# A transformer layer (linear attention with decay, and an expert-mixed linear layer) on eight cores: V weights by another queue, the decay set-up later, k scaled a slot ahead, and a split last chunk

## What is computed

```python
xn = layernorm(x)
# attention: H = 8 heads of DK = 64
q = phi(xn @ W_Q.T); k = phi(xn @ W_K.T); v = xn @ W_V.T       # phi(u) = elu(u) + 1
S = gamma * S + k_t v_t^T;  z = gamma * z + k_t                # per token and head
out_t = (S q_t) / (z q_t + 1e-6)
y = (out * sigmoid(xn @ W_g.T + b_g)) @ W_O.T
# linear layer with low-rank experts: 8 experts of rank 4, the best 2
f = xn @ W_lin.T + b_lin + sum_k softmax_weight_k * (xn @ left_k) @ right_k
return x + y + f
```

## Time and profile before

| | us |
|---|---|
| median of 3 runs (lowest, highest) | 260.21 (259.84, 260.92) |
| the profiled execution | 260.27 |
| its span, the slowest core (core 3) | 259.2 |
| span of the other cores | 256.0 to 258.8 |
| TensorE busy | 236.6 (91%) |
| VectorE, ScalarE, POOL busy | 162.0, 75.5, 61.7 |
| granted clock of TensorE, all cores | 1.000 |

### The profile page before, as it was taken

How to read it: one execution, slowest core, us unless ns; L and a number is a source line. 1 busy time by engine, 2 the same in 40 slices (tenths; PEclk the granted TensorE clock), 3 DMA queues, 4 the chain that set the end, 5 groups by cost and what they waited for, 6 DMA issues and landing times.

```text
span 259.2 us, 5279 instructions; the slowest of 8 cores (256.0 to 259.2 us)
## 1 busy us (share of the span) xinstructions
PE 236.6 (91%) x1688; PEld 116.9 (45%) x1688; DVE 162.0 (63%) x425; ACT 75.5 (29%) x128; POOL 61.7 (24%) x99
## 2 busy tenths in 40 slices
PE   0238999999989999999999999999999999999995
PEld 0124354454545555454444455444545454445442
DVE  3743667658848678666555657556656776677522
ACT  2653766476163432314132021112110201000000
POOL 0790300012144421405050403021304030333000
PEclk9999999999999999999999999999999999999999
DMA  5999999999998046342435122223231315243423
GB/s 147 237 153 263 250 167 188 252 174 177 232 199 266 3 116 192 61 164 61 164 41 170 37 82 83 101 82 104 82 124 63 121 63 181 82 153 104 154 106 137
DMA packets 20366, 35.86 MB, mean 138 GB/s; under 512 B 12210, under 2 KB 12530, under 8 KB 20084
## 3 DMA queue, kind: packets, MB, share of 16 engines
q1 hardware_dynamic: 17444, 24.89, 32.0%
q0 software_dynamic: 2896, 10.64, 21.7%
HBM read 32.00 MB, written 8.39 MB: 156 GB/s over the span
## 4 chain that ended last, share of the span: by engine, by line
PE 85%; DMA 6%; DVE 3%; issue 2%; ACT 2%; DVEq 0%; ACTq 0%; POOLq 0%
PE PJ L367 27%; PE L L389 17%; PE L L433 9%; PE PJ L360 8%; DMA wv_sb<-wv 5%; PE PJ L389 4%; PE L L367 3%; PE PJ L433 2%; PE SY L381 2%; DMA x_sb<-x 2%; PE SY L405 2%; PE T L419 1%; PE SY L409 1%; PE T L338 1%; PE T L427 1%
## 5 line engine op out<-in xcount | busy, mean ns | idle before, releaser
L389 PE MATMUL L<-wlin_sb,xnfm 128*128 128x512 bf16 x208 | 49.2, 379 | 0.0
L325 POOL TENSOR_SCALAR S_blk<-S_sb,small_s 128x260 bf16<-128x260 f32 x30 | 28.6, 969 | 82.7 <-DVE S_sb L827 82.5
L389 PEld LDWEIGHTS L<-wlin_sb,xnfm 128*128 128x128 bf16 x208 | 20.0, 98 | 24.4 <-issue 1.0
L656 DVE TENSOR_SCALAR e_sb<-e_sb 128x512 bf16<-128x512 bf16 x32 | 9.7, 302 | 30.7 <-ACT e_sb L898 30.7
L898 ACT ACTIVATE e_sb<-PJ 128x512 bf16<-128x512 f32 x28 | 16.5, 593 | 40.5 <-PE PJ L367 39.4
L367 PE MATMUL PJ<-xnfm,wk_sb 128*128 128x512 bf16 x112 | 26.6, 380 | 1.2 <-ACT th_g L905 1.2
L874 ACT ACTIVATE xn_tm<-x_sb,nmr,rstd 128x1024 bf16<-128x1024 f32 x16 | 19.9, 1242 | 25.4 <-POOL nmr L281 23.9
L433 PE MATMUL L<-wo_sb,ygfm 128*128 128x512 bf16 x104 | 26.7, 379 | 0.0
L367 PE MATMUL PJ<-xnfm,wg_sb 128*128 128x512 bf16 x112 | 26.6, 379 | 0.0
L367 PE MATMUL PJ<-xnfm,wq_sb 128*128 128x512 bf16 x112 | 26.6, 380 | 0.0
L360 PE MATMUL PJ<-wv_sb,xnfm 128*128 128x512 bf16 x96 | 23.7, 389 | 2.5 <-DMA wv_sb<-wv 2.5
(11 more groups left out here) (122 smaller groups left out, 336.7 us busy)
## 6 DMA issues: line engine op xcount, KB each, us to landing
ro_sb<-x SPq DMA_DIRECT2D x16, 512.0 KB, 3.4
out<-ro_sb SPq DMA_DIRECT2D x15, 512.0 KB, 2.7
x_sb<-x SPq DMA_DIRECT2D x10, 512.0 KB, 8.4
x_sb<-x POOLq DMA_DIRECT2D x6, 512.0 KB, 21.6
wlin_sb<-wlin POOLq DMA_DIRECT2D x1, 2048.0 KB, 38.5
wv_sb<-wv POOLq DMA_DIRECT2D x4, 256.0 KB, 12.7
wq_sb<-wq POOLq DMA_DIRECT2D x2, 512.0 KB, 18.5
wk_sb<-wk POOLq DMA_DIRECT2D x2, 512.0 KB, 25.4
```

The costliest lines, as they stand in the source:

```text
L325: GP.tensor_scalar(S_blk[:, :].rearrange("p (q w) -> p q w", q=4)[:, :, 65 * e : 65 * e + 65], S_sb[:, :].rearrange("p (q w) -> p q w", q= ...
L389: TE.matmul(lb(c, n)[:, :], xnk(k, c), wlin_sb[:, D * k + 512 * n : D * k + 512 * n + 512], start=False, stop=False)
L656: VE.tensor_scalar(e_sb[:, 512 * i : 512 * i + 512], e_sb[:, 512 * i : 512 * i + 512], 1.0, None, ALU.min).then_inc(dv_m, 1)
```

## The change

1. **V's weights.** V is loaded uncast, in two halves, by SyncE's queue, into the space of `wlin_sb` (seen as f32), between and behind x chunks 2 and 3. VectorE casts it in four pieces into `wv_sb` (`cast_wv`, semaphore `dv_cast`). POOL waits for the first half before it issues the load of Q's first half. W_lin, whose space is borrowed, waits for the four casts; its load and that of W_O are issued ahead of `gC` and `dpk` instead of behind. TensorE takes V's matmuls in another order.
2. **The decay set-up** is spread behind the V and Q work: the mask exponents behind the last Q feature, `dpq` behind the Q exps, `masks` behind the normalisation of chunk 7. The statistics of chunks 4 and 5 come earlier.
3. **k scaled a slot ahead.** From slot 4 on, unless a block begins, `ktm_sb` of chunk c+1 is computed in slot c, ahead of the gate multiply.
4. **Output sums.** In slots 13 to 15 the second output sum of the chunk c-3 stands behind the masks, instead of at the end of the slot before.
5. **The last chunk** is computed in parts of 512, 256 and 256 columns, in the banks PJ0, PJ1 and SY0, with a sum and a store each.

```diff
+LAST = ((0, 512), (512, 256), (768, 256))
...
+    wv32 = wlin_sb[:, :].bitcast(F32)
...
+        def load_wv(hf):
+            o = 4 * FH * hf
+            SY.dma_start(wv32[:, o : o + 4 * FH],
+                         wv_d[:, o : o + 4 * FH]).then_inc(d_wv[hf], 16)
+
         load_x(0)
         load_x(1)
         SY.dma_start(ident[:, :], ident_d[:, :]).then_inc(d_id, 16)
         load_x(2)
+        load_wv(0)
         load_x(3)
+        load_wv(1)
...
     def pool_program():
         GP.memset(mhalf[:, :], -0.5).then_inc(po_ini, 1)
-        GP.wait_ge(d_x[0], 16)
-        for i in range(4):
-            o = 2 * FH * i
-            GP.dma_start(wv_sb[:, o : o + 2 * FH], wv_d[:, o : o + 2 * FH]).then_inc(d_wv[i], 16)
+        GP.wait_ge(d_wv[0], 16)
         wload_half(wq_sb, wq_d, 0, d_wq)
...
+        GP.wait_ge(dv_cast, 4)
+        wload(wlin_sb, wlin_d, d_wl)
+        wload(wo_sb, wo_d, d_wo)
         GP.wait_ge(po_ini, 1)
         GP.wait_ge(ac_dec, 3)
...
-        wload(wlin_sb, wlin_d, d_wl)
-        wload(wo_sb, wo_d, d_wo)
...
+    def last_part(c, o, w, bank):
+        n = o // 512
+        ro_ = ((c // 4) % 2) * 512 + 128 * (c % 4)
+        TE.matmul(bank[:, 0:w], thr[64 * n : 64 * n + 64, ro_ : ro_ + 128],
+                  right_sb[64 * n : 64 * n + 64, o - 512 * n : o - 512 * n + w],
+                  start=True, stop=False)
+        for k in range(KCH):
+            TE.matmul(bank[:, 0:w], xnk(k, c), wlin_sb[:, D * k + o : D * k + o + w],
+                      start=False, stop=False)
+        for j in range(4):
+            ins = TE.matmul(bank[:, 0:w], yg(c)[:, 128 * j : 128 * j + 128],
+                            wo_sb[:, D * j + o : D * j + o + w],
+                            start=False, stop=(j == 3))
+        ins.then_inc(pe_o, 1)
...
+    def cast_wv(i):
+        o = 2 * FH * i
+        VE.wait_ge(d_wv[i // 2], 16)
+        VE.tensor_copy(wv_sb[:, o : o + 2 * FH], wv32[:, o : o + 2 * FH]).then_inc(dv_cast, 1)
...
+            if c < 4 or s == 0:
+                ktm(c)
+            if c == 0:
+                VE.wait_ge(ac_mk, 1)
             VE.wait_ge(pe_sc, c + 1)
             VE.tensor_tensor(A_sb[:, 0:512], SYb[0][:, :], masks[:, 0:512], ALU.mult)
             VE.tensor_tensor(A_sb[:, 512:1024], SYb[1][:, :], masks[:, 512:1024],
                              ALU.mult).then_inc(dv_mask, 1)
+            if c > NCH - 4:
+                outv(lo - 1, 1)
...
             if c < NCH - 1:
                 qt(c + 1)
+            if c >= 4 and s < 3:
+                ktm(c + 1)
...
-            if lo >= 0:
+            if lo >= 0 and (c < NCH - 4 or c == NCH - 1):
                 outv(lo, 1)
```

More of the change, by code:

```diff
@@ L129, in build_core @@
     ring4 = [PJ[0], PJ[1], L[0], L[1]]
+    lastb = [PJ[0], PJ[1], SYb[0]]
     sem = nc.alloc_semaphore
@@ L138, in build_core @@
     d_lg = sem("d_lg")
-    d_wv, d_wq, d_wk, d_wg = ([sem(f"d_wv{i}") for i in range(4)], [sem("d_wqa"), sem("d_wqb")],
+    d_wv, d_wq, d_wk, d_wg = ([sem("d_wva"), sem("d_wvb")], [sem("d_wqa"), sem("d_wqb")],
                               [sem("d_wka"), sem("d_wkb")], [sem("d_wga"), sem("d_wgb")])
@@ L145, in build_core @@
     pe_av, pe_st, pe_ytr, pe_o = sem("pe_av"), sem("pe_st"), sem("pe_ytr"), sem("pe_o")
+    dv_cast = sem("dv_cast")
     dv_ini, dv_st, dv_bn, dv_xev = sem("dv_ini"), sem("dv_st"), sem("dv_bn"), sem("dv_xev")
@@ L251, in sp_program @@
         c = NCH - 1
-        for n in range(2):
+        for n, (o, w) in enumerate(LAST):
             SY.wait_ge(dv_out, 2 * c + n + 1)
-            SY.dma_start(out_d[128 * c : 128 * c + 128, 512 * n : 512 * n + 512],
-                         ro(c)[:, 512 * n : 512 * n + 512]).then_inc(d_o[c], 16)
+            SY.dma_start(out_d[128 * c : 128 * c + 128, o : o + w],
+                         ro(c)[:, o : o + w]).then_inc(d_o[c], 16)
         for c in range(NCH - 1):
             SY.wait_ge(d_o[c], 16)
-        SY.wait_ge(d_o[NCH - 1], 32)
+        SY.wait_ge(d_o[NCH - 1], 16 * len(LAST))
     def wload(dst, srcd, s):
@@ L486, in pe_program @@
         TE.wait_ge(dv_xev, 1)
+        for i in range(2):
+            TE.wait_ge(dv_cast, i + 1)
+            vproj(0, ring4[0], 2 * i, 2 * i + 2)
         xtr(2)
         TE.wait_ge(dv_xev, 2)
[L489 to L498, removed]
+        vproj(1, ring4[1], 0, 4)
+        TE.wait_ge(dv_xev, 3)
+        vproj(2, ring4[2], 0, 4)
+        for i in range(2, 4):
+            TE.wait_ge(dv_cast, i + 1)
+            vproj(0, ring4[0], 2 * i, 2 * i + 2)
+        xtr(3)
+        vproj(1, ring4[1], 4, 8)
+        vproj(2, ring4[2], 4, 8)
+        TE.wait_ge(dv_xev, 4)
+        vproj(3, ring4[3])
         TE.wait_ge(d_wq[0], 16)
@@ L629, in pe_program @@
                 gproj(c)
[L630 to L634, removed]
+        lo = NCH - 2
+        right_pair(lo)
+        for n in range(2):
+            lin_group(lo, n)
+            o_group(lo, n)
+        lo = NCH - 1
+        TE.wait_ge(dv_out, 2 * lo - 2)
+        TE.wait_ge(ac_thr, NB)
+        TE.wait_ge(dv_norm, NCH)
+        TE.wait_ge(dv_gate, NCH)
+        for i, (o, w) in enumerate(LAST):
+            last_part(lo, o, w, lastb[i])
     def stats(c):
@@ L711, in top2b, with ktm @@
         VE.tensor_copy(t3[:, :, 64 : 64 + ER], t3[:, :, 0:ER]).then_inc(dv_th, 1)
+    def ktm(c):
+        if c < 4:
+            VE.wait_ge(pe_ktr, c + 1)
+            ktile = KT[c]
+        else:
+            VE.wait_ge(d_kt[c // 4], 64)
+            ktile = kts(c // 4)[:, 512 * (c % 4) : 512 * (c % 4) + 512]
+        if c > 0:
+            VE.wait_ge(pe_st, c)
+        VE.tensor_tensor(ktm_sb[:, :], ktile, dpk[:, :], ALU.mult).then_inc(dv_ktm, 1)
     def outv(lo, n):
@@ L734, in dve_program @@
         xev_v(0)
+        cast_wv(0)
+        cast_wv(1)
+        xev_v(1)
         stats(3)
-        xev_v(1)
         xev_v(2)
+        cast_wv(2)
+        cast_wv(3)
         xev_v(3)
+        stats(4)
         VE.wait_ge(d_sm, 16)
         VE.tensor_scalar(gb_h[:, :], small[:, 0:4], 0.5, None, ALU.mult).then_inc(dv_ini, 1)
+        stats(5)
         VE.wait_ge(ac_dec, 1)
         VE.tensor_scalar(nlg[:, :], nlg[:, :], 1e15, None, ALU.min).then_inc(dv_dec, 1)
+        xev_v(4)
+        for m in range(2):
+            phi(m, ring4[m], fm(qfm, 0)[:, 512 * m : 512 * m + 512], dv_q)
         VE.wait_ge(ac_dec, 2)
@@ L745, in dve_program @@
                          ALU.mult).then_inc(dv_dec, 1)
+        xev_v(5)
+        for m in range(2, 4):
+            phi(m, ring4[m], fm(qfm, 0)[:, 512 * m : 512 * m + 512], dv_q)
         VE.wait_ge(d_cm, 16)
@@ L752, in dve_program @@
         ins.then_inc(dv_mk, 1)
[L753 to L760, removed]
         stats(6)
         stats(7)
-        VE.wait_ge(ac_mk, 1)
+        VE.wait_ge(ac_dec, 3)
         qt(0)
@@ L846, in dve_program @@
                 top2a(b + 1)
-            if lo >= 0:
+            if lo >= 0 and (c < NCH - 4 or c == NCH - 1):
                 outv(lo, 1)
-        for lo in range(NCH - LAG, NCH):
-            outv(lo, 0)
-            outv(lo, 1)
+        outv(NCH - 2, 0)
+        outv(NCH - 2, 1)
+        lo = NCH - 1
+        for i, (o, w) in enumerate(LAST):
+            VE.wait_ge(d_r[lo], 16)
+            VE.wait_ge(pe_o, 2 * lo + i + 1)
+            VE.tensor_tensor(ro(lo)[:, o : o + w], lastb[i][:, 0:w],
+                             ro(lo)[:, o : o + w], ALU.add).then_inc(dv_out, 1)
     def xn(c):
@@ L925, in act_program @@
             xn(c)
+        for c in range(4):
+            vev(c, ring4[c])
+        xn(4)
         SE.wait_ge(dv_ini, 4)
         SE.activation(nlg[:, :], small[:, 4:16], AF.Exp, scale=-1.0).then_inc(ac_dec, 1)
+        xn(5)
         SE.wait_ge(dv_dec, 1)
         SE.activation(nlg[:, :], nlg[:, :], AF.Ln, bias=one_c[:, :]).then_inc(ac_dec, 1)
+        for m in range(4):
+            SE.wait_ge(pe_q, m + 1)
+            eexp(m, ring4[m])
         SE.wait_ge(dv_dec, 2)
@@ L937, in act_program @@
         ins.then_inc(ac_dec, 1)
[L938 to L946, removed]
         vev(4, ring4[0])
@@ L950, in act_program @@
         xn(7)
+        SE.wait_ge(dv_mk, 1)
+        SE.activation(masks[:, :], mtmp, AF.Exp).then_inc(ac_mk, 1)
         for m in range(4):
```

## The result

The changed kernel takes **261.85 us** (median of 6 runs, 261.62 to 262.54), the kernel before 259.78 us (6 runs, 259.24 to 260.92): ratio 1.0083, 95% interval 1.0059 to 1.0108. It is slower by 0.8%; the forecast was no change. The time lies inside the stated range, but between the forecast itself (up to 261.5 us) and rival 2 (263.0 us). A ratio rests on the times of all runs and need not be the quotient of the two medians. One run each of the last chunk not split (number 3) and of the chain early again (number 9) took 299 us with a far lower clock on some cores of one die, and is left out of the ratios. The profiled execution took 261.78 us.

The account below looks back on a forecast made before the run. With TensorE busy 91% of the span, its start and the end were taken to count: front end +1.8 us, tail -1.9 us, sum -0.1 us on the profiled 260.27 us, giving 260.2 us; range 257.9 to 262.9 us.

Parts of the forecast that it names:

- rival 2: Between K and gate matmuls: clock falls to 1.2 GHz in the new gap, +2.8 us, 263.0 us; chance 0.16.
- V and Q's start: Front end: V's weights by SyncE's queue, casts of 0.7 us, Q starting at 26.0 us, 2.7 us earlier.
- First Q exp: Front end: first exp of the Q features at 32.9 us, decided by chunk 4's landing, 1.7 us earlier.
- The decay chain: Between Q and K features: mask exponents and exps moved there lose their cover and cost 3.5 us.
- The clock: Between K and gate matmuls: the sum kept the front's +1.8 us unchanged up to the slots, without a clock fall.
- The sign set for it: Gate matmuls: 0.43 us each would show the forecast wrong.
- The tail: Slots 13 to 15 and the end: -1.9 us, bounds -1.3 and -2.6.
- The k multiply and the sums: Slots 13 to 15: three waits of 0.42 us at the masks go, 1.3 us gained.
- The split: Last chunk: same matmul columns, shorter last sum and last store, 0.3 us less each.
- Rival 1: Start: loads run earlier, chunk 4 at 24.3 us, first Q exp 31.4 us, time 258.7 us; chance 0.27.
- Rival 3: Start: V's second half late, 262.0 us, or casts hold up POOL's loads by 1.4 us, 261.6 us; chance 0.15.

Follow-up runs that it names:

- number 3: Changed kernel with the last chunk in two parts of 512 columns as before: 261.26 us, ratio 1.0070 to the kernel before.
- number 9: Repeat of the changed kernel with the decay chain early, spread between V's evictions: 256.55 us, ratio 0.9875 to the kernel before.
- numbers 1 and 5: 1: changed kernel with the decay chain early, between V's evictions, 256.21 us, ratio 0.9873; 5: kernel before with only the decay chain moved, 265.58 us, ratio 1.0180.
- the filler: Changed kernel with 13 unused 512-column matmuls on TensorE between K and the gate matmuls: 259.78 us, ratio 1.0006 to the kernel before.
- number 4: Kernel before with only V's weights by SyncE's queue, the casts and V's new order on TensorE: 261.19 us, ratio 1.0060.
- numbers 5 to 8: Kernel before plus: 5 chain moved, 1.0180; 6 k multiply and sums, 0.9910. Changed kernel, chain early: 7 no split, 0.9908; 8 rank-path matmuls together, 0.9881.
- number 7: Changed kernel with the decay chain early between V's evictions and the last chunk in two parts: 258.41 us, ratio 0.9908 to the kernel before.

## Why the prediction was wrong

Most of its steps hold. Its sum left out the fall of the clock and had three terms of the wrong size, and one of these hid part of the loss.

- **V and Q's start.** Casts of 0.65 us (0.7 taken), on core 7 the second half at 19.3 us (19.7) and chunk 4 at 25.1 us (25.8), Q's start at 25.6 us (26.0). Right.
- **First Q exp.** Forecast at 32.9 us on the slowest core, 1.7 us earlier. It came at 31.89 us there, 2.75 us earlier. The 1.77 us of the mean are no hit, since their base is a mean first exp of 33.13 us and the forecast's was 34.6. VectorE began chunk 4 0.7 us earlier than taken, and from there to the exp it was 6.7 us instead of 7.1. The reason given, that chunk 4 decides and not Q's start, holds on five cores, the slowest among them (6.7 us behind chunk 4); on cores 2, 3 and 5 the exp follows Q's start by 6.1 us. This miss of 1.0 us was to the good: without it the kernel would be near 262.9 us (an estimate), the very end of the range.
- **The decay chain.** +3.50 us between the two exps on every core; 3.5 forecast. Right, and shown from both sides (numbers 1 and 5).
- **The clock: the step that failed.** The sum went on without it ("so the 1.8 us stay") and left it to rival 2, with a chance of 0.16. The gap came much as that rival had it: from 44.3 to 49.0 us on core 7, with two waits of 3.5 us in all and transposes between. The sign set for it came too, gate matmuls of 0.43 us each, on six of eight cores, and there the argument against it, the transposes in the middle, did not hold. Its price was 2.8 us; measured, by the time from the gate matmuls to slot 0's scores, it is 0.9 to 1.3 us on five cores, 2.2 us on core 7 and nothing on cores 0 and 5, 1.01 us in the mean. The prediction calls TensorE's 1.2 us for the tanh its only wait behind Q's start, though the earlier trace rows has four shorter ones, of up to 0.4 us, as well. The price took all 16 matmuls of the gate's first half at the lower level; on those five cores about 7 or 8 of them ran at it, on core 7 thirteen, until 54.4 us. In the kernel's time the filler puts it at 2.0 us, since the slowest core counts. The Trainium skill (TensorE: Matmul & The Clock Gate, Part 1) says that an idle stretch brings the clock back to the lower state; by that rule the rival was the forecast, and on six of eight cores the trace now agrees, though no wait in the gap was longer than 2.02 us. On cores 0 and 5 it doesn't agree, with the same 2.02 us of wait.
- **The tail.** -1.9 us forecast, -1.49 measured. The k multiply and the sums gave 1.7 us instead of 1.3: slots 13 and 14 went from 7.46 us to 7.01 and 6.89 on core 7, and with k and the sums only 0.5 us more came behind them (mean); I had counted the wait at the masks alone. Where the rest comes from in each slot wasn't taken apart. The split was mis-sized with its sign: "the matmul columns are the same" is true, but each part needs its own 64-row matmul, and the two further ones cost TensorE 0.7 us. It lost 0.1 to 0.2 us (41.97 against 41.84 and 41.75 us) where 0.6 of gain was forecast.
- **Rival 1** (loads earlier) came in part. VectorE, which waited for both, started on V's second half at 18.9 us and on chunk 4 at 24.5 us in the mean, and the first Q exp was at 31.36 us; the rival had 18.7, 24.3 and 31.4 us. The slowest core lay between it and the forecast. Its time, 258.7 us, did not come, because the clock fell. **Rival 3** (loads late) did not come. POOL's first load of W_Q took 0.90 us to issue next to the casts, on all eight cores, and 0.57 or 0.58 us before, so a cast can hold up POOL, but by 0.3 us. The Trainium skill has such a rule (SBUF — State Buffer, on DVE blocking DMA); its effect is there, and small.

By the marks of the slowest core: forecast -0.1 us, found +1.5 us. The difference of 1.6 us, which is also that between 260.2 and 261.85 us, is the clock (2.25) and the tail (0.4), less the 1.0 us of the earlier first Q exp. So it is partly luck that the time lies well inside the range: two misses pulled in opposite directions. In the mean span, +1.26 us, the clock is 1.01 us; core 7 was the one with the longest fall.

## What to carry to other kernels

When a change opens a gap on TensorE, price the gap twice, by its length and by what the matmuls behind it cost at the lower level, and if the rows can't exclude it, put the second into the sum. Moving work off one waiting place is only half of an edit: ask which idle time on the same engines is nearest, here the pauses between V's evictions, and put it there. An edit can be a loss by itself and still be part of a gain, so undo one part at a time before judging the whole: V's early start lost 0.6% by itself, and is part of a version that is 1.5% faster. Where the time is that of the slowest core, forecast and measure on that core: a mean can agree by chance.

## What the runs showed of the hardware

- The clock's fall isn't a plain function of the waits of a core. Cores 0, 1 and 5 of the changed kernel had nearly the same two waits (1.19, 0.98 and 0.97 us, then 2.02 us), and only core 1 went to the lower level. Cores 0 and 5 kept the higher one. In number 4 all eight cores had one wait of 2.6 us, and three fell. On the chip of numbers 5 to 8 a mean clock of 0.996 or less shows on 5 of 96 core spans of the kernel before too, and on 12 of 56 in number 7. What tells them apart stays open.
- Matmuls without use can shorten a kernel: 13 of them, 2.8 us of TensorE's time at the higher level, gave back 2.0 us.
- A load may be issued long before its first byte: POOL's first half of W_Q was issued at 15.15 us on core 7, and its queue showed no packet until 18 us.
- SyncE's queue moved 0.99 MB from 12 to 15 us on core 7 (330 GB/s, 98.8% busy), and 0.84 MB in a stretch as busy before (280 GB/s). Half of the 0.99 MB are rows of 4 KB, the size of x's, and half rows of 8 KB, V's, so the higher rate isn't that of V's rows alone.
